# ALiBi bias as exact bf16 parts, four 64-column products per tile, and the scatters of the second FFN spread over its blocks

## What is computed

```
pos = arange(N);  diff = pos[None, :] - pos[:, None];  diff = where(diff > 0, 0.0, diff)
attn = einsum('bhqd,bhkd->bhqk', q, k) * SCALE + diff[None] * slopes[:, None, None] * 8.0
w = softmax(attn);  x = x + proj(w @ v)
x = x + 0.5 * ffn(layernorm(x))          # before the attention and after it
```

## Time and profile before

| | |
|---|---|
| median of three runs | 482.72 us (482.23 to 482.81) |
| the profiled execution | 483.79 us, of which span 481.9 us |
| instructions | 10906 |
| PE, matmul | 429.5 us busy, 89% of the span |
| DVE | 313.0 us, 65% |
| ACT | 238.3 us, 49% |
| POOL | 236.7 us, 49% |
| mean granted PE clock | 0.982 of full speed |

### The profile page before, as it was taken

One profiled execution on the slowest core, in us unless ns is written; L12 is line 12 of the kernel. 1 busy time (PEld: TensorE's weight loads), 2 busy tenths in 40 slices (PEclk: granted clock), 3 DMA queues, 4 the chain that ended last, 5 costly groups with the idle time before them and its releaser, 6 DMA issues.

```text
span 481.9 us, 10906 instructions
## 1 busy us (share of the span) xinstructions
PE 429.5 (89%) x3447; PEld 367.0 (76%) x3447; DVE 313.0 (65%) x935; ACT 238.3 (49%) x585; POOL 236.7 (49%) x321
## 2 busy tenths in 40 slices
PE   1999989989999898699999899999888999999890
PEld 0888877878899775477777677777658998889780
DVE  3776877868776583485859486857546666544662
ACT  3745543444434556255656547464665544444441
POOL 7367796645543314134454353514345568644341
PEclk9999999989999999899999899999999999999996
DMA  8971121214231101130212111110022223223522
GB/s 241 300 122 57 50 84 37 66 53 110 62 91 36 52 24 38 53 88 24 59 49 59 43 46 41 50 42 23 14 93 63 65 69 102 61 68 109 150 76 78
DMA packets 50633, 35.51 MB, mean 74 GB/s; under 512 B 5754, under 2 KB 47706, under 8 KB 50538
## 3 DMA queue, kind: packets, MB, share of 16 engines
q1 hardware_dynamic: 45140, 23.90, 19.3%
q0 software_dynamic: 4784, 10.54, 6.4%
q10 hardware_dynamic: 656, 0.40, 0.3%
HBM read 15.37 MB, written 13.01 MB: 59 GB/s over the span
## 4 chain that ended last, share of the span: by engine, by line
PE 47%; issue 6%; DMA 5%; DVE 5%; ACT 5%; POOL 4%; ACTq 1%; SPq 1%; POOLq 0%; DVEq 0%
PE bank L1490 6%; PE bank L1586 5%; PE bank L1625 4%; PE bank L1610 4%; PE bank L1472 3%; PE bank L1483 3%; PE bank L1473 3%; PE bank L1474 3%; PE bank L1589 3%; PE bank L1590 2%; POOL yp L538 2%; PE bank L1613 2%; PE bank L1614 2%; DMA qk_rows<-wd 2%; ACTq L870 1%
## 5 line engine op out<-in xcount | busy, mean ns | idle before, releaser
L538 POOL DMA_INDIRECT yp<-scr,dest x77 | 76.6, 995 | 84.3 <-ACT scr L770 71.4
L1263 DVE TENSOR_REDUCE nm<-bank 128x2 f32<-128x512 f32 x128 | 84.0, 685 | 44.1 <-PE bank L1590 42.1
L877 ACT ACTIVATE stage<-bank 128x512 f32<-128x512 f32 x128 | 74.1, 596 | 70.9 <-PE bank L1614 65.0
L1490 PE MATMUL bank<-wd,scr 128*128 (+1 forms) x462 | 65.3, 278 | 1.3 <-ACT scr L763 1.3
L1154 DVE TENSOR_TENSOR scr<-bank,scr 128x352 f32<-128x352 f32 x77 | 40.2, 522 | 37.6 <-ACT scr L783 36.9
L763 ACT ACTIVATE scr<-bank 96x128 f32<-96x128 f32 x77 | 21.0, 273 | 87.4 <-DVE scr L1137 85.1
L1472 PE MATMUL bank<-wu,xbT 128*128 x154 | 56.3, 366 | 6.0 <-DVE scr L1154 3.4
L1490 PEld LDWEIGHTS bank<-wd,scr 128*128 128x128 f32 (+1 forms) x462 | 58.2, 193 | 2.0 <-issue 1.7
L1586 PE MATMUL bank<-qk_rows 126*128 126x256 bf16 x256 | 51.1, 282 | 4.6 <-DMA qk_rows<-lev 4.1
L1610 PE MATMUL bank<-qk_rows 128*128 128x256 bf16 x256 | 50.3, 279 | 4.0 <-DMA qk_rows<-wd 3.2
L1474 PE MATMUL bank<-wu,xbT 128*128 x154 | 50.0, 325 | 0.0
(11 more groups left out here) (218 smaller groups left out, 956.7 us busy)
## 6 DMA issues: line engine op xcount, KB each, us to landing
qk_rows<-lev SPq DMA_DIRECT2D x96, 64.0 KB
scr<-xs SPq DMA_DIRECT2D x77, 64.5 KB, 1.8
stage<-yp SPq DMA_DIRECT2D x8, 256.0 KB, 4.5
scr<-yp SPq DMA_DIRECT2D x6, 256.0 KB, 3.2
stage<-in_w SPq DMA_DIRECT2D x8, 176.0 KB, 3.6
stage<-in_v SPq DMA_DIRECT2D x8, 176.0 KB, 4.8
xs<-qk_rows SPq DMA_DIRECT2D x3, 451.5 KB, 9.7
yp<-scr,dest POOLq DMA_INDIRECT x77
```

The lines of the kernel that those rows point to most:

```text
L538: nc.gpsimd.indirect_dma_start(out=yp[PHASE[n]][:, :], out_offset=bass.IndirectOffsetOnAxis(ap=dest[:, n:n + 1], axis=0), in_=ysb[:, n % Y ...
L877: nc.scalar.activation(probs[:, g % RING, kt, 2 * (hp % 2):2 * (hp % 2) + 2, :], psS2[(b * 16 + j) % 3][:, :].rearrange("p (h n) -> p h n" ...
L1263: nc.vector.tensor_reduce(nm[:, qt, 2 * hp:2 * hp + 2], psS1[i % 2][:, :].rearrange("p (h n) -> p h n", h=2), AX.X, ALU.max, negate=True). ...
L1490: i = nc.tensor.matmul(ph[n % len(ph)][:, 3 * P:4 * P], hTs[0:w, n % 2, k * P:(k + 1) * P], wd[0:w, bass.ds(experts[n], 1), k, :].rearrang ...
```

## The change

1. The rows now hold more of the bias: 42 rows of q and k, six (`FAR` to `FAR + 5`) for each of the seven borders between blocks of 32 positions. The slope is split in three bf16 parts that add up to it exactly, and each is paired with small integers, which bf16 holds exactly. What is left is the bias within a block of 32, which `near` adds with four bf16 products of 64 columns (32 positions x two heads), 96 rows deep, in place of the two F32R products.
2. Everything for it is made on chip: positions by ten iotas on POOL (`places`), parts of the slope by eleven small operations of POOL (`slope_parts`), `row_slopes` by ACT (16 of 96 x 256), integers on DVE (`row_steps`, `near_parts`, `row_integers`, `near_integers`), all in the dense stage. The loads of `dist`, `far` and `slope_col`, `far_*`, `near_high`, `near_low` and `idn_r` are gone.
3. SP lays the rows with 39 DMAs, 4 at each of the blocks n = 0 to 8 and 3 at n = 9, where it had 17 at n = 0 to 7. Before the first it waits for the zeroed rows (POOL's six memsets, L649), `row_integers` and the 16 `row_slopes`.
4. In the second FFN, the eight scatters of batches 6 and 7 go one by one to i = 2, 4, ..., 16, the zero scatters to i = 18 and 20, the bias adds to i = 22 to 25.

```diff
+LW = 32
+LB, LQ, LP = N // LW - 1, P // LW, 3 * LW
+LATE_ROWS = {2 + 2 * j: (j // 2, j % 2) for j in range(8)}
+LATE_ZEROS = {18: [0], 20: [1]}
+def bias_rows(n):
+    return range(4 * n, min(4 * n + 4, 13 * RING)) if n < 10 else range(0)
```

On SP, in `between_blocks`:

```diff
                 if n == 0:
-                    sp.wait_ge(wu_lo_done, 1)
-                    sp.dma_start(far_v, far).then_inc(far_landed, 16)
...
+                    sp.wait_ge(zero_done, 2 * RING)
+                    sp.wait_ge(ints_done, 3)
+                    sp.wait_ge(row_slopes_done, H)
+                for j in bias_rows(n):
+                    bias_row(j // 13, j % 13)
...
+            def bias_row(i, j):
...
+                part, to = j // 2 % 3, FAR + j // 2
+                q_to, k_to = [x[i][to:to + SPREAD * (LB - 1) + 1:SPREAD, :, :] for x in (qs, ks)]
+                if j < 6:
+                    if j % 2:
+                        sp.dma_start(k_to, row_slopes[LW * part + LB + 1:LW * part + 2 * LB + 1]).then_inc(rows_landed, 16)
+                    else:
+                        sp.dma_start(q_to, row_ints[0:LB, 0, None, :].broadcast_to([LB, H, N])).then_inc(rows_landed, 16)
```

On POOL, in the dense stage:

```diff
             for c in range(4):
                 rstd_of(0, c, 4 * c, 4)
+                if c == 2:
+                    places()
...
             nc.gpsimd.tensor_scalar(slope8[:, :], slope8[:, :], 8.0, None, ALU.mult).then_inc(slope_done, 1)
+            slope_parts()
```

On POOL, in the second FFN:

```diff
-            scatter2(B - 2)
             for n in range(FIRST[1], sum(NB)):
                 y_scatter(n)
...
-                if 8 <= i < 10:
-                    scatter2(B - 1, [NT - 2 + i - 8])
-                if i == 10:
-                    zero_scatter(2)
-                if 12 <= i < 16:
-                    add_ffn_bias(1, i - 12)
+                if i in LATE_ROWS:
+                    t, k = LATE_ROWS[i]
+                    scatter2(B - 2 + t // TB, [NT - 4 + t], [k])
+                if i in LATE_ZEROS:
+                    zero_scatter(2, LATE_ZEROS[i])
+                if 22 <= i < 26:
+                    add_ffn_bias(1, i - 22)
```

On ACT, in the dense stage:

```diff
                 if i >= 8:
-                    for j in (2 * (i - 8), 2 * (i - 8) + 1):
-                        near_high(j // H, j % H)
+                    row_slope(i - 8)
```

On DVE, between the blocks, and the operations that `near_integers` makes:

```diff
-                for j in near_parts(n):
-                    near_low(j // H, j % H)
...
+            def near_integers(x):
+                if x == 0:
+                    nc.vector.tensor_scalar(in_tile[:, 0], at_tile[:, :, :], LW - 0.5, -1.0, ALU.is_lt, ALU.mult).then_inc(ints_done, 1)
+                else:
+                    nc.vector.tensor_scalar(in_tile[:, 1], at_tile[:, :, :], 0.0, None, ALU.is_ge).then_inc(ints_done, 1)
+                dve.wait_ge(ints_done, x + 4)
+                nc.vector.scalar_tensor_tensor(near_ints[:, x], at_near[:, :, :], 0.0, in_tile[:, x], ALU.min if x else ALU.max,
+                                               ALU.mult).then_inc(near_done, 1)
```

On DVE, in the dense stage:

```diff
+                if i == 5:
+                    row_steps()
+                if i == 6:
+                    near_parts()
+                if i == 15:
+                    row_integers()
+                if i in (18, 22):
+                    near_integers((18, 22).index(i))
```

On PE, in `scores_1` (in `scores_2` the same with `x` = 1 and `kt`):

```diff
-                o = o[:, :].rearrange("p (h n) -> p h n", h=2)[:, :, qt * P:(qt + 1) * P]
-                nc.tensor.matmul(o, idn_r[:, :], near_hi[0][:, 2 * hp:2 * hp + 2, :], start=False, stop=False)
-                nc.tensor.matmul(o, idn_r[:, :], near_lo[0][:, 2 * hp:2 * hp + 2, :], start=False, stop=True).then_inc(s1_full, 1)
+                near(o, 0, qt, hp).then_inc(s1_full, 1)
+
+            def near(o, x, tile, hp):
+                o = o[:, :].rearrange("p (h n) -> p h n", h=2)
+                for a in range(LQ):
+                    at = tile * P + a * LW
+                    i = nc.tensor.matmul(o[:, :, at:at + LW], near_ints[:, x, a, :], near_slopes[:, 2 * hp:2 * hp + 2, :],
+                                         start=False, stop=(a == LQ - 1))
+                return i
```

More of the change, by code:

```diff
@@ L521, in rstd_of, with scatter @@
                 nc.gpsimd.tensor_tensor(nmr[:, t], nmr[:, t], rstd[:, t], ALU.mult).then_inc(nmr_done[w], 1)
-            def scatter(r, c, src, landed, tiles=None):
+            def scatter(r, c, src, landed, tiles=None, copies=range(2)):
                 T = CHUNKS[r][0]
@@ L529, in scatter @@
                 for t in tiles or range(c * T, (c + 1) * T):
-                    for k in range(2):
+                    for k in copies:
                         nc.gpsimd.indirect_dma_start(
@@ L630, in _, with places @@
             nc.gpsimd.tensor_scalar(tri8[:, :, :], tri8[:, :, :], 0.0, None, ALU.is_ge).then_inc(pool_const, 1)
+            def places():
+                for p in range(3):
+                    at = slice(LW * p, LW * p + LW)
+                    for k, (to, pattern, base, step) in enumerate(((at_row[at, :], [[1, N]], -LW, -LW), (at_diag[at, :], [[1, LW]], 0, -1),
+                                                                   (at_near[at, :, :], [[-LW, LQ], [1, P]], 0, -1))):
+                        if p or k:
+                            pool.wait_ge(at_done, 3 * p + k)
+                        else:
+                            pool.wait_ge(nmr_done[0], 3)
+                        nc.gpsimd.iota(to, pattern, base=base, channel_multiplier=step, allow_small_or_imprecise_dtypes=True
+                                       ).then_inc(at_done, 1)
+                pool.wait_ge(at_done, 9)
+                nc.gpsimd.iota(at_tile[:, :, :], [[-LW, LQ], [1, P]], base=0, channel_multiplier=0,
+                               allow_small_or_imprecise_dtypes=True).then_inc(at_done, 1)
@@ new lines, in slope_parts @@
+            def slope_parts():
+                pool.wait_ge(slope_done, 1)
+                nc.gpsimd.tensor_copy(slope_b[:, :], slope8[0:LP, :]).then_inc(part_step, 1)
+                pool.wait_ge(part_step, 1)
+                nc.gpsimd.tensor_copy(slope_part[:, :], slope_b[:, :]).then_inc(part_step, 1)
+                for p in (1, 2):
+                    for k, at in enumerate([slice(LW * x, LW * x + LW) for x in range(p, 3)]):
+                        first = 2 + 3 * k if p == 1 else 8
+                        pool.wait_ge(part_step, first)
+                        nc.gpsimd.tensor_tensor(slope_rest[at, :], (slope8 if p == 1 else slope_rest)[at, :], slope_part[at, :],
+                                                ALU.subtract).then_inc(part_step, 1)
+                        pool.wait_ge(part_step, first + 1)
+                        nc.gpsimd.tensor_copy(slope_b[at, :], slope_rest[at, :]).then_inc(part_step, 1)
+                        pool.wait_ge(part_step, first + 2)
+                        nc.gpsimd.tensor_copy(slope_part[at, :], slope_b[at, :]).then_inc(part_step, 1)
+                pool.wait_ge(part_step, 11)
```

146 lines of the change are left out of this document (66 added, 80 removed).

## The result

The changed kernel takes 492.8 us (median of four, 491.27 to 498.66) against 482.62 (now also of four): a ratio of 1.0161 with an interval of 1.0108 to 1.0215, slower by 1.6%. The forecast was 465, with a range up to 476. The profiled execution of the changed kernel is the slowest of its four, 498.66 with a mean clock of 0.947; a second profile of it (e0_after, clock 0.950) shows the same waits in the same places.

The account below looks back on a forecast made before the run. The prediction took PE as the bound in mid-batch attention, DVE close behind and taking over once units shorten. Its terms, 4.0 - 5.5 - 1.5 - 14.0 - 0.8 = -17.8 us, took the median 482.7 to 464.9 (predicted 465, range 452 to 476).

Parts of the forecast that it names:

- part 3: blocks(0): near_low's removal gains 5.5 us, shorter scores_1(0) units 1.5; SP's row DMAs cost nothing, hidden by prefetch.
- Rival (e): Start of the blocks: rows late on SP or DVE's table stalls; most gain given back, 476 to 484 us; chance 0.05.
- Rival (a): Whole kernel: PE bounds everywhere and DVE packs behind it; 34.9 us off, 448 us; chance 0.12.
- Rival (b): Dense stage: DVE caught between bias adds and memsets, +12 us in place of +4, 473 us; chance 0.15.
- part 4: Dense stage: later POOL work and first near_integers operations cost 2.1 us, near_integers(1) beside memsets 1.9; together +4.0.
- Part 1: Attention scores: four products of 64 columns make a unit 0.35 us, not 0.47; 30.7 us less PE work.
- rival d: Scores: each small product costs its load, 0.096 us, so the kernel is slower than before, 518 us; chance 0.05.
- Part 2: Attention: of 30.7 us less PE work 15.5 reach the end, less 1.5 for the clock: -14.0 us.
- Rival (c): Attention: shorter PE work drops to 1.2 GHz after each batch's start, 473 us; chance 0.10.
- part 5: Second FFN: spread scatters leave room for DVE's dest copies; -0.8 us (-2.5 to +1.5).

Follow-up runs that it names:

- e0_after: The changed kernel run once more with no edit, as base of the other runs: 496.34 us.
- e3_both: The changed kernel with the row DMAs spread over all 31 blocks and near_integers(1) moved between the blocks: 472.43 us (0.9767 of the kernel before).
- e2_rows: The changed kernel with the 39 row DMAs spread over all 31 blocks and counted per set of rows: 474.24 us (0.9777 of the kernel before).
- e1_hold: The changed kernel with near_integers(1) moved from dense step i = 22 to between the blocks (n = 2): 492.93 us (1.0122 of the kernel before).
- e6_near1: e3_both with one product of 64 columns in place of four: 467.82 us (0.9638 of the kernel before).
- e9_both_again: The kernel of e3_both unedited, run again for five rounds on one chip: 472.52 us (0.9749 of the kernel before).
- e7: e3_both with POOL's scatters, zero scatters and bias adds of the second FFN where the kernel before had them: 475.7 us (0.9804).
- e10: The kernel of e7 run again, on one chip with e9_both_again: 473.27 us (0.9767 of the kernel before).
- e4: e2_rows with the first operation of near_integers(1) written with two SBUF inputs in place of one: 470.93 us, a single execution.
- e11: The kernel of e4 run again, on one chip with e9_both_again: 472.63 us (0.9766 of the kernel before).

## Why the prediction was wrong

The forecast of 464.9 missed by 27.9 us. 20.4 of them, from 492.80 down to e3_both's 472.43, go with the two places ahead of attention; the other 7.5 are mostly gain in attention that did not come.

**The step that failed** stands in part 3: "SP is therefore nearly full with rows and the blocks' own loads, which run some blocks ahead; I cost it at nothing, hidden by this prefetch. Without it, up to 0.3 a block for ten blocks, 3 us." In max_T of batch 0 it cost 18.0 us (e0_after against e2_rows), or 20.8 with the hold out of the way (175.73 in e1_hold against 154.98 in e3_both), and the rows at hand allowed a better sum. Three things were wrong in it. The DMA was priced at the stack's 0.64; the broadcasts and strided rows take 0.73 to 0.97. Four of them were set against a block's 2.6 us by themselves, without the block's own load (0.35) and the gap at each group. And a prefetch only delays: once SP needs 13.05 us for what PE wants every 7.7 (46.28 / 6, the pace before), ten blocks of it are 10 / 3 x 5.35 = 17.8 us late. That this comes so near to 18.0 is partly luck. PE waited only 12.0 us for loads in e0_after, since the product leaves the blocks loaded ahead out, and the clock adds a loss that the product doesn't have: (1 - 0.88) x 101.28 = 12.2 us up to max_T where e2_rows loses (1 - 0.96) x 83.24 = 3.3.

**Rival (e)** named this mechanism, with a chance of 0.05 and a price of 476 to 484. Its place was right; its price was too low (the change took 492.8), and its chance too. **Rival (a)**, PE as the bound everywhere, is refuted by the 7.2 us that attention gained of 30.7. **Rival (b)** had DVE caught between bias adds and memsets: it was caught by the memsets alone, and that cost 2.7 to 5.4 us at max_T (part 4), not 12.

**Part 4** was wrong in both of its terms, the first in its sign and the second in its size. The first operations of `near_integers` don't delay the dense stage: the block table now ends before POOL's bias adds start (L1094 takes 0.18 us at 63.15, against 3.06), because these are later by 3.8 us while DVE is not. DVE reaches the `dense_hid` of 71.26 about 1 us earlier than before. But the hold of `near_integers(1)`, for which I took a value between "free" and 3.3 us, was 8.2 (8.60 less the 0.40 of L1269): I put the operation at 74 us and it came at 71.86, and I had the memsets end at 77.6 and they ended at 80.2 (POOL's eleven small operations took 3.0 us, about as reckoned, but the first scatter came 2.0 later and not 1.0). In the time, removing the hold brought 2.7 us at max_T with the rows in the way and 5.4 without them (160.41 to 154.98). A delay hidden behind a greater one is only partly paid, so neither number is "the" cost.

**Part 1 was right:** 0.34 us a unit against 0.35 forecast. The runs with eight products and with one bear the price out: units of 0.45 and 0.25 us, so 0.03 for each product more or less. Neither price that spoke against it holds here: not the load alone (0.096 each, rival d), and not the 81 ns for each pair that the Trainium skill, "TensorE: Matmul & The Clock Gate", section "Back-to-back issue gap", states for 128 columns. That figure may hold for 128 columns, which no run here tried; at 64 columns and bf16 the pitch is 30 ns, in groups of four and of eight.

**Part 2 was right in kind and too large:** 14.0 forecast for attention (13.2 without batch 7, which comes behind the last mark), 7.2 and 7.8 measured between the marks. By batch, from one max_T to the next, e3_both gains 0.8, 0.6, 0.1, 1.1, 3.6, 1.8 and -0.3; I had 1.5, 2.2 and then 2.2 each. Of the 3.6, 1.7 is a stretch of low clock that only the kernel before had there. Two terms of the sum were missized. The first is the clock: I added one stretch, 1.5 us, and e3_both has three more than the kernel before, 5.1 us, of which 3.4 fall in batch 1's step, that of the 0.6. At most 3.6 of the missing 5.4 us are that; PE also waited in these batches, so not all of it need reach the end. The second is the middle of a batch: the three steps in which neither kernel has a low stretch, the first, the fourth and the sixth, gain 0.8, 1.1 and 1.8 where I had 1.5, 2.2 and 2.2. I took PE's 13.6 and DVE's 13.81 and added 1.0 for packing; but work of DVE that comes in bursts (the rotation and the row maxima behind it, six of them in 3.88 us at 274.32 in e3_both) seems not to move forward, and the products that wait for ACT appear as soon as PE arrives early. That this is the reason is read from the waits; no run moved a slot, so it is argued and not shown. That PE's work alone isn't the limit is shown by e6_near1, clock included; how the rest divides between clock, DVE and ACT is open.

**Rival (c)** holds in part. In `blocks(0)` the low clock is part of the loss: the mean of 0.88 over 100.99 us is 12.1 us of full clock not granted, against (1 - 0.98) x 80.30 = 1.6 before, some of it while PE waited anyway. The falls come with the long waits, and in e3_both, without these waits, the clock is 1.00. In attention the change has four low stretches that cost 1.7 us each, e3_both has five and the kernel before two.

**Part 3's gain and part 5.** With the rows spread and the hold gone, max_T of batch 0 comes 2.5 us earlier than before; the forecast for all ahead of it was 4.0 - 5.5 - 1.5 = -3.0. The 2.22 us wait at 101.75 is gone. Part 5's -0.8 lies within what was measured (0.75 and 3.3), which is too wide to call it confirmed. The holds that it spoke of are gone: in the second FFN of the change no `dest` (L1177) takes over 0.23 us, where two took 1.82 and 1.63 before.

## What to carry to other kernels

A DMA queue is an engine: add up everything that one pass of the loop issues on it, the loop's own loads and gaps too, and divide by the pace of the loop; what is over is lost on each pass, and a prefetch can give back only what it had loaded ahead. The same 39 DMAs cost 18 us at four a block and nothing measurable when spread, so when a change adds work to a queue ask first how late each piece may come.

When the bound of a stage moves off an engine, take a small share of the work removed (here a quarter of 30.7 us, low clock included), unless another bound has been worked out slot by slot.

## What was unexpected of the hardware

A held DVE operation can stay held through several POOL operations in a row: L1271 waited from 71.86 to 80.46 through the rest of six memsets of 1.76 us each, with no turn in between. How long differs from one execution to the next of the same kernel: the copy `dest` inside the same run of memsets took 1.46 us in e3_both and 5.25 in e9_both_again, 5.80 and 1.61 in e7 and e10, 5.22 and 2.70 in e4 and e11. Each time it ended where a memset ended. What decides which one was not tried.

The changed kernel varies from 488 to 499 us among its executions, and the repaired ones from 468 to 478, where the kernel before keeps within 0.6 to 6 us in a set of runs. Their profiles show more stretches at half clock, of about 1.7 us lost each; that these make the spread is not shown.
